# Twelve key maxima and an expert's downward matmuls gathered at each gelu of the third feed-forward layer

## The chip, the cores and the metric

The kernel runs on one core of a Trainium2 chip. The metric is the time of one execution on the device, in microseconds (us). One core has TensorE (PE, matrix products), VectorE (DVE), ScalarE (ACT), GpSimd (POOL), and SyncE (SP), which here only issues DMA transfers. Each engine works through its own list of instructions in order; they meet at semaphores.

## The reference

Four layers are applied one after the other to 1024 tokens of width 128. Each has a cross attention over 6404 context rows (16 heads of 8 channels) and then a mixture of 8 experts, of which a token uses two:

```
x = x + attention_l(layernorm(x), context)      l = 0, 1, 2, 3
x = x + experts_l(layernorm(x))
attention: softmax(q k / sqrt(8)) v  for l = 0, 1, 3;  sigmoid(q k / sqrt(8)) v  for l = 2
experts, l = 2:
  comb = one_hot(top 2 of softmax(x @ router_w + router_b)), weighted
  for e in range(8):
      h = gelu(x @ expert_up[e].T)              # 128 -> 512, not approximate
      out = out + comb[:, e] * (h @ expert_down[e].T)
experts, l = 0, 1, 3: silu(x @ a) * (x @ b), then downward
```

## The kernel before

The tokens are cut into two blocks of 512, so there are 8 units of work: unit u is layer u // 2, block u % 2. The attention of a unit is done in 4 phases of 4 heads each, 32 phases in all. A phase walks over 51 tiles of 128 keys. For each key tile TensorE forms two score pairs (`score`, each two heads in two PSUM banks), ScalarE turns each pair into `prob` (`exp`: Exp, or Sigmoid in layer 2), and one tile later TensorE multiplies them with V (`av`, four heads). I count time in key tiles: a tile (24, 36) is tile 36 of phase 24, and its length is the time from its first `exp` to that of the next tile.

A softmax phase needs, beforehand, the maximum of each query's scores. These maxima of phase p + 1 are found during phase p: 176 pieces (`max` on TensorE into a bank of the three `side` banks, `red` on VectorE). 32 of them (`both`) work on a difference of two key chunks that TensorE and ScalarE prepared (`dif`, `relu`). They are handed out by `find`, which keeps a running sum of planned VectorE time (`spent`) in step with the position in the phase.

The experts of unit u - 1 are worked off as background while unit u attends. For layer 2 that is `pass_steps` with `gated` false: pass 4 (unit 4, during phases 20 to 22, Sigmoid, no maxima) and pass 5 (unit 5, during phases 24 to 26, Exp, with maxima). An expert k has four upward products (`up`, 128x512 out of Fin), each copied into a hidden buffer (`upc`: by VectorE in pass 4, where `by_dve` is true, by ScalarE in pass 5), a `gelu` over all four (one 128x2048 instruction, line 978), a multiplication with the routing weight on GpSimd (`hscale`, two instructions, line 1316, with the weight row in `cwb`), and four accumulating downward products (`down`, line 870), added up by `ysum` (in pass 5 by way of a ScalarE copy, `yc`). Two experts' gelus stand side by side, so that ScalarE loads the gelu table once for both and then loads its attention table again.

The order of all instructions is written out beforehand. `placed` gives every background step a position: a position is a quarter of a key tile, `gap` is the distance to the step before it, and a TensorE step takes a position of its own in each key tile, so eight `up` and eight `down` between two pairs of gelus take 16 tiles. `attention_steps` then lays scores, maxima and background steps into one list, and each engine takes its own steps from it in that order.

Weights: `wexp` fetches an expert's Fin and Fout (256 KB each, lines 1400 and 1401) into a ring of 3. The fetch for expert k + 3 waits until `down` of expert k has read its slot (line 1397), and `up` of expert k + 3 waits for it (line 847). `cwget` fetches the weight row of expert k + 2 into `cwb` once `hscale` of expert k is done (line 1413). Both are issued by SP, one after the other in the order of the list.

Of the kernel before, what the change touches and what calls it, by code (L numbers as in the profile page):

```python
# [7 lines left out]
ACT = mybir.ActivationFunctionType  # L8
# [29 lines left out]
E = 8  # L38
# [74 lines left out]
def softmax(l):  # L113
    return l != 2


def unit(u):

    return u // 2, u % 2
# [7 lines left out]
def by_dve(u, lp):  # L127

    return u in (3, 4, 7)
# [7 lines left out]
Step = namedtuple("Step", "eng what key")  # L137
# [138 lines left out]
def pass_steps(u, lp):  # L276

    l, b = unit(u)
    f = FFN[l]
    out = [(6, Step("PE", "logit", (u, lp)))]  # L280
    out += [(3 if what == "routea" else 2, Step("DVE", what, (u, lp))) for what in ("routea", "routeb", "routee", "routef", "routeg", "routeh")]
    out += [(2, Step("ACT", "rexp", (u, lp)))]
    out += [(4 if what == "routej" else 2, Step("DVE", what, (u, lp))) for what in ("routej", "routek", "routel")]
    if l == 0:
        out += [(2, Step("DVE", "routec", (u, lp))), (6, Step("PE", "count", (u, lp)))]
    out += [(2, Step("DVE", "routed", (u, lp))), (4, Step("PE", "cwT", (u, lp))), (1, Step("ACT", "cwTc", (u, lp))),
            (2, Step("SP", "cwput", (u, lp)))]
    for k in range(W_RING):
        out.append((0, Step("SP", "wexp", (u, lp, k))))
    out.append((0, Step("SP", "cwget", (u, lp, 0))))  # L290
    if f["gated"] and l != 3:
        out.append((0, Step("POOL", "xk", (u, lp, 0))))
    out.append((16, None))
    n = f["nk"]

    def down(k, c):
        out.append((1, Step("PE", "down", (u, lp, k, c))))
        if c == n - 1:
            if by_dve(u, lp):
                out.append((3, Step("DVE", "ysum", (u, lp, k))))  # L300
            else:
                out.append((0, Step("ACT", "yc", (u, lp, k))))
                out.append((0, Step("POOL", "ysum", (u, lp, k))))
            if k + W_RING < E:
                out.append((0, Step("SP", "wexp", (u, lp, k + W_RING))))

    def gated(k, j):
        out.append((1, Step("PE", "up", (u, lp, k, j))))
        out.append((0, Step("ACT", "tanh", (u, lp, k, j))))
        if l == 3 or not by_dve(u, lp):  # L310
            out.append((0, Step("ACT", "ac", (u, lp, k, j))))
        out.append((1, Step("PE", "up", (u, lp, k, n + j))))
        if by_dve(u, lp):
            out.append((2, Step("DVE", "gatea", (u, lp, k, j))))
            out.append((0, Step("DVE", "gateb", (u, lp, k, j))))
        else:
            out.append((0, Step("ACT", "gc", (u, lp, k, j))))
            out.append((0, Step("POOL", "gatea", (u, lp, k, j))))
            out.append((0, Step("POOL", "gateb", (u, lp, k, j))))
        if l == 3:  # L320
            out.append((0, Step("POOL", "gatec", (u, lp, k, j))))
        if j == 0 and k + 1 < E and l != 3:
            out.append((0, Step("POOL", "xk", (u, lp, k + 1))))

    if not f["gated"]:
        out.append((0, Step("SP", "cwget", (u, lp, 1))))
    for k in range(E):
        if f["gated"]:
            if k + 1 < E:
                out.append((0, Step("SP", "cwget", (u, lp, k + 1))))  # L330
            for j in range(n):
                gated(k, j)
            if k:
                for c in range(n):
                    down(k - 1, c)
            continue
        for j in range(n):
            out.append((1, Step("PE", "up", (u, lp, k, j))))
            out.append((3, Step("DVE", "upc", (u, lp, k, j))) if by_dve(u, lp) else (0, Step("ACT", "upc", (u, lp, k, j))))
            if k > 1:  # L340
                down(k - 2, j)
        if k % 2:
            out += [(0, Step("ACT", "gelu", (u, lp, i))) for i in (k - 1, k)]
            for i in (k - 1, k):
                out += [(0, Step("POOL", "hscale", (u, lp, i, j))) for j in range(2)]
                if i + 2 < E:
                    out.append((0, Step("SP", "cwget", (u, lp, i + 2))))
    out.append((8, None))
    for k in range(E - 1 if f["gated"] else E - 2, E):
        for c in range(n):  # L350
            down(k, c)
    out += [(6, Step("PE", "yT", (u, lp))), (3, Step("DVE", "yadd", (u, lp)))]
    return out
# [27 lines left out]
    return out  # L381


def placed(at, steps, taken):


    out = []
    for gap, s in steps:
        at += gap
        if s is not None and s.eng == "PE":  # L390
            at += (1 - at) % 4
            while at in taken:
                at += 4
            taken.add(at)
        if s is not None:
            out.append((at, s))
    return out


def loads(u):  # L400
# [3 lines left out]
    if b:  # L404
# [5 lines left out]
        if l == 3:  # L410
# [6 lines left out]
            ysum=0.7, upc=0.7)  # L417
# [5 lines left out]
def attention_steps(units):  # L423
# [4 lines left out]
    for p in range(first, last + 1):  # L428
        at = p * Q
# [13 lines left out]
    for u in units:  # L443
        at = NG * u * Q
        if u:
            back += placed(at + 16, finish_steps(u - 1), taken)
    for u in units:
        l, b = unit(u)
        at = NG * u * Q
# [5 lines left out]
    def window(p):  # L455

        return max(first * Q, (p - 1) * Q - LEAD), p * Q - LEAD

    out = []
    n = 0  # L460
    p = first + 1
    spent, single, both, ready, ahead, total = 0.0, [], [], [], [], None

    def find(half, t, most):

        nonlocal spent
        a, e = window(p)
        for _ in range(most):
            if t < e - 8 and spent >= total * (t + 1 - a) / (e - 8 - a):
                return  # L470
            if both[half] and (ready[half][0] <= t if ready[half] else False):
                i = both[half].pop(0)
                if both_of(ITEM_DIF[i])[1] == i:
                    ready[half].pop(0)
                spent += COST["both"]
            elif single[half]:
                i = single[half].pop(0)
                spent += COST["red"]
            else:
                return  # L480
            out.append(Step("PE", "max", (p, i)))
            out.append(Step("DVE", "red", (p, i)))

    for t in range(first * Q, (last + 1) * Q):
        kt, q = t // 4 % KT, t % 4
        if t >= window(p)[1]:
            assert total is None or not (single[0] or single[1] or both[0] or both[1] or ahead)
            p, total = p + 1, None
        has = p <= last + 1 and p < 32 and softmax(phase(p)[0]) and t >= window(p)[0]
        if has and total is None:  # L490
            a, e = window(p)
            half_of = len(HALVES[0])
            spent, single = 0.0, [list(range(0, half_of)), list(range(half_of, FIRST_BOTH))]
            both = [[i for i in range(FIRST_BOTH, len(ITEMS)) if ITEMS[i][2] // 2 == half] for half in range(2)]
            ready = [[], []]
            ahead = [(a + (e - 24 - a) * d // len(DIFS), d) for d in range(len(DIFS))]
            total = FIRST_BOTH * COST["red"] + (len(ITEMS) - FIRST_BOTH) * COST["both"]
            total += sum(COST.get(s.what, 0.15) for at, s in back if s.eng == "DVE" and a <= at < e - 8)
        if q in (0, 2):
            half = q // 2  # L500
            out.append(Step("PE", "score", (t // Q, kt, half)))
            out.append(Step("ACT", "exp", (t // Q, kt, half)))
            if has:
                find(1 - half, t, 2 if t < window(p)[1] - 8 else 5)
        if q == 3:
            if kt:
                out.append(Step("PE", "av", (t // Q, kt - 1)))
            elif t // Q > first:
                out.append(Step("PE", "av", (t // Q - 1, KT - 1)))
            if has:  # L510
                find(0 if len(single[0] + both[0]) > len(single[1] + both[1]) else 1, t, 1)
            if has and ahead and ahead[0][0] <= t and not ready[0] and not ready[1]:
                d = ahead.pop(0)[1]
                out.append(Step("PE", "dif", (p, d)))
                out.append(Step("ACT", "relu", (p, d)))
                ready[DIFS[d][1]].append(t + 5)
        while n < len(back) and back[n][0] <= t:
            s = back[n][1]
            out.append(s)
            if s.eng == "DVE":  # L520
                spent += COST.get(s.what, 0.15)
            n += 1
    out.append(Step("PE", "av", (last, KT - 1)))
    out.append(Step("ACT", "drain", (last,)))
# [1353 lines left out]
```

## Time and profile before

| | us |
|---|---|
| median of 3 runs | 4747.94 (4747.63 to 4750.8) |
| the profiled execution, its own time | 4733.75 |
| its span, first to last instruction | 4731.8 |
| TensorE busy | 3965.9 |
| ScalarE busy | 3983.6 |
| VectorE busy | 2803.3 |
| GpSimd busy | 829.8 |
| mean granted TensorE clock | 0.953 of full speed |

Busy times are unions over an engine's instructions. The time beside "span" is what a run of the kernel takes; the profiled execution was 14 us below the median of the three timed runs.

### The profile page before, as it was taken

What the parts mean: (1) busy time and instruction counts of PE and PEld (TensorE: products, weight loads), DVE (VectorE), ACT (ScalarE), POOL (GpSimd) and SP (SyncE); (2) the same over time, 40 slices, a digit from 0 to 9 for tenths busy, and PEclk for the clock granted to TensorE, in tenths of its full rate; (3) what the DMA queues carried; (4) which work ended last, traced back from release to release, by engine and by line L of the source; (5) the groups of instructions that cost most, each with busy time, mean ns of one, the idle gap of its engine ahead of it and who ended that gap; (6) DMA issues with size and microseconds to landing.
All of it is one profiled execution on the core that took longest, in us unless ns stands there. A gap on an engine that the chain in (4) does not pass through costs nothing. (4 is left out here: it accounts for less than half of the span.)

```text
span 4731.8 us, 68983 instructions
## 1 busy us (share of the span) xinstructions
PE 3965.9 (84%) x26742; PEld 911.7 (19%) x26742; DVE 2803.3 (59%) x5598; ACT 3983.6 (84%) x4403; POOL 829.8 (18%) x719
## 2 busy tenths in 40 slices
PE   3578888888888888888898999888888888888887
PEld 2112111111112221122112222111111111122112
DVE  1487888778877778877610111011287568886833
ACT  2478998889978898888899888978998888888994
POOL 3001000340014410143522011012001120035002
PEclk7579999999989999999999999999999999999998
DMA  2212000110002110011102121100001100011001
GB/s 73 84 42 56 20 13 18 31 29 10 13 26 56 30 47 10 19 47 35 37 13 61 37 74 40 35 31 26 13 13 36 32 13 13 14 32 32 10 1 47
DMA packets 105922, 150.33 MB, mean 32 GB/s; under 512 B 23064, under 2 KB 64032, under 8 KB 105584
## 3 DMA queue, kind: packets, MB, share of 16 engines
q1 hardware_dynamic: 105584, 145.82, 10.9%
q8 instruction: 213, 3.49, 0.3%
q14 instruction: 125, 1.02, 0.1%
HBM read 122.24 MB, written 23.51 MB: 31 GB/s over the span
## 5 line engine op out<-in xcount | busy, mean ns | idle before, releaser
L913 ACT ACTIVATE prob<-scores 128x1024 f32<-128x1024 f32 x3264 | 3177.3, 1025 | 274.4 <-PE scores L748 259.6
L1022 DVE TENSOR_REDUCE mpart<-side 128x1 f32<-128x512 f32 (+1 forms) x3312 | 2039.4, 656 | 707.8 <-PE side L779 697.5
L758 PE MATMUL av<-prob,VB 128*9 128x512 f32 x6528 | 873.3, 607 | 1.3 <-ACT prob L913 0.5
L758 PE MATMUL av<-prob,VA 128*9 128x512 f32 x6528 | 869.5, 605 | 1.7 <-ACT prob L913 0.8
L748 PE MATMUL scores<-QP,KA 32*128 32x512 f16 x3264 | 640.7, 393 | 195.2 <-ACT above L921 118.2
L748 PE MATMUL scores<-QP,KB 32*128 32x512 f16 x3264 | 630.5, 388 | 195.0 <-ACT above L921 94.2
L779 PE MATMUL side<-KB,QP 32*128 32x512 f16 (+1 forms) x2112 | 583.8, 385 | 43.0 <-DVE mpart L1022 29.1
L779 PE MATMUL side<-KA,QP 32*128 32x512 f16 (+1 forms) x1936 | 534.0, 378 | 33.3 <-DVE mpart L1022 19.4
L1026 DVE CUSTOM_DVE_ANT_0 above<-side,above 128x512 f32<-128x512 f32 x736 | 493.0, 685 | 69.9 <-PE side L779 68.1
L921 ACT ACTIVATE above<-scores 128x1024 f32<-128x1024 f32 x368 | 376.8, 1024 | 169.1 <-PE scores L770 118.1
L748 PEld LDWEIGHTS scores<-QP,KB 32*128 32x128 f16 x3264 | 151.8, 91 | 867.7 <-ACT prob L913 538.6
L748 PEld LDWEIGHTS scores<-QP,KA 32*128 32x128 f16 x3264 | 151.8, 91 | 818.8 <-ACT prob L913 437.0
L779 PEld LDWEIGHTS side<-KB,QP 32*128 32x128 f16 x2112 | 140.2, 91 | 591.3 <-DVE mpart L1022 452.5
L779 PEld LDWEIGHTS side<-KA,QP 32*128 32x128 f16 x1936 | 130.8, 91 | 522.2 <-DVE mpart L1022 389.3
L852 PE MATMUL scores<-xnT,Fin 128*128 128x512 f32 (+1 forms) x256 | 147.5, 659 | 45.1 <-ACT above L921 31.7
L870 PE MATMUL side<-hT,Fout 128*128 128x512 f32 (+1 forms) x304 | 172.1, 653 | 8.0 <-POOL hT L1316 4.2
L1233 POOL TENSOR_TENSOR o_tok<-o_tok,bvo 128x512 f32<-128x512 f32 x6 | 7.6, 1272 | 890.5 <-DVE o_tok L1054 491.3
L1294 POOL TENSOR_TENSOR ag<-ag 128x512 f32<-128x512 f32 (+1 forms) x80 | 101.5, 1269 | 330.2 <-ACT ag L967 330.2
L1343 POOL CAST hi<-kb 128x512 f16<-128x512 f32 (+1 forms) x60 | 35.7, 596 | 626.3 <-ACT kb L997 625.8
L1524 DVE TENSOR_REDUCE mpart<-side 128x1 f32<-128x512 f32 (+1 forms) x80 | 49.3, 633 | 144.6 <-PE side L1476 144.6
L758 PEld LDWEIGHTS av<-prob,VA 128*9 128x9 f32 x6528 | 96.9, 88 | 192.4 <-issue 184.8
L758 PEld LDWEIGHTS av<-prob,VB 128*9 128x9 f32 x6528 | 97.0, 88 | 192.0 <-issue 184.5
(200 smaller groups left out, 2787.3 us busy)
## 6 DMA issues: line engine op xcount, KB each, us to landing
cwb<-weights SPq DMA_DIRECT2D x80, 256.0 KB, 3.8
KA<-kstacks SPq DMA_DIRECT2D x192, 96.0 KB
KB<-kstacks SPq DMA_DIRECT2D x192, 96.0 KB
Fin<-in_Fin SPq DMA_DIRECT2D x64, 256.0 KB, 2.8
kstacks<-hi SPq DMA_DIRECT2D x112, 128.0 KB, 2.4
ctxc<-in_ctxT SPq DMA_DIRECT2D x48, 256.0 KB, 3.0
kstacks<-lo SPq DMA_DIRECT2D x56, 128.0 KB, 2.6
hT<-in_mask SPq DMA_DIRECT2D x16, 400.2 KB, 3.3
```

Of the source, the lines that this page charges most:

```text
L748: last = pe.matmul(pair[:, j, :], K[p % 2][rows(h), kt * P:kt * P + P], QP[p % 3][rows(h), :], start=True, stop=True)
L758: last = pe.matmul(AV[ROWS * h:ROWS * h + VC, :], V[l % 2][:, kt, g * HG + h, :], prob[:, (e + h // 2) % RING, (h % 2) * QB:(h % 2) * QB + ...
L779: pe.matmul(bank[:, 0:chunk_of(c)], QP[p % 3][rows(h), qt * P:(qt + 1) * P], K[p % 2][rows(h), chunk(c)], start=True, stop=True).then_inc( ...
L852: pe.matmul(bank[0:fs, :], Fin[:, w, j * fs:(j + 1) * fs], x[:], start=True, stop=True).then_inc(sem["bgP"], 1)
L870: pe.matmul(bank, Fout[0:fs, w, c, :], h, start=first, stop=c == nk - 1).then_inc(sem["bgP"], 1)
L913: act.activation(prob[:, e % RING, :], pair.rearrange("p a b -> p (a b)"), ACT.Exp if softmax(l) else ACT.Sigmoid, scale=SCALE).then_inc(s ...
L921: act.activation(above[:].rearrange("p a b -> p (a b)"), pair.rearrange("p a b -> p (a b)"), ACT.Relu).then_inc(sem["bgA"], 1)
L1022: dve.tensor_reduce(part, bank, AX.X, ALU.max).then_inc(sem["red"], 1)
L1026: dve.tensor_tensor_reduce(more, bank, more, 1.0, LEAST, ALU.add, ALU.max, part).then_inc(sem["red"], 1)
L1294: pool.tensor_tensor(a, a, g, ALU.mult).then_inc(sem["bgG"], 1)
L1343: pool.tensor_copy(hi16[:, slot, 0:w], k).then_inc(sem["bgG"], 1)
L1524: dve.tensor_reduce(mpart[:, qt, h, c:c + 1], MX[:, n_max % 2, 0:chunk_of(c)], AX.X, ALU.max).then_inc(sem["red"], 1)
```

## The change

Three things are changed in the written order; no instruction is added or taken away, and no tile or buffer changes. First, after a pair of gelus the `down` products of expert k - 2 are placed at the same position as the gelus (`SAME`), behind them, where they had been spread among the `up` of expert k. Second, in pass 4 (`by_dve`) the four `up` of expert k + 1, with their copies, are placed there too, behind those `down`, and the `down` of expert k - 1 then follow one per key tile. Third, after each gelu at a time when maxima are being looked for (pass 5) six maxima are handed out at once, three from each half of the heads, whatever the running sum says.

```diff
-    def down(k, c):
-        out.append((1, Step("PE", "down", (u, lp, k, c))))
+    def down(k, c, gap=1):
+        out.append((gap, Step("PE", "down", (u, lp, k, c))))
         if c == n - 1:
             if by_dve(u, lp):
-                out.append((3, Step("DVE", "ysum", (u, lp, k))))
+                out.append((3 if gap > 0 else 0, Step("DVE", "ysum", (u, lp, k))))
...
-        for j in range(n):
-            out.append((1, Step("PE", "up", (u, lp, k, j))))
-            out.append((3, Step("DVE", "upc", (u, lp, k, j))) if by_dve(u, lp) else (0, Step("ACT", "upc", (u, lp, k, j))))
-            if k > 1:
-                down(k - 2, j)
+        if k % 2 or not k or not by_dve(u, lp):
+            for j in range(n):
+                out.append((1, Step("PE", "up", (u, lp, k, j))))
+                out.append((3, Step("DVE", "upc", (u, lp, k, j))) if by_dve(u, lp) else (0, Step("ACT", "upc", (u, lp, k, j))))
+                if k % 2 == 0 and k:
+                    down(k - 2, j)
         if k % 2:
             out += [(0, Step("ACT", "gelu", (u, lp, i))) for i in (k - 1, k)]
             for i in (k - 1, k):
                 out += [(0, Step("POOL", "hscale", (u, lp, i, j))) for j in range(2)]
                 if i + 2 < E:
                     out.append((0, Step("SP", "cwget", (u, lp, i + 2))))
+            if k > 1:
+                for j in range(n):
+                    down(k - 2, j, SAME)
+            if k + 1 < E and by_dve(u, lp):
+                for j in range(n):
+                    out += [(SAME, Step("PE", "up", (u, lp, k + 1, j))), (0, Step("DVE", "upc", (u, lp, k + 1, j)))]
+                for j in range(n):
+                    down(k - 1, j)
...
+SAME = -1
...
     for gap, s in steps:
+        if gap == SAME:
+            out.append((at, s))
+            continue
         at += gap
...
-    def find(half, t, most):
+    def find(half, t, most, now=False):
...
-            if t < e - 8 and spent >= total * (t + 1 - a) / (e - 8 - a):
+            if not now and t < e - 8 and spent >= total * (t + 1 - a) / (e - 8 - a):
                 return
...
             if s.eng == "DVE":
                 spent += COST.get(s.what, 0.15)
+            if s.what == "gelu" and has:
+                find(0, t, 3, True)
+                find(1, t, 3, True)
```

## Rows read from the trace of the kernel before

**Rows 1.** The page, part 1, and part 5: engine, operation, tiles, count | busy us, mean ns | idle before it.
```profile
PE 3965.9 (84%) x26742; PEld 911.7 (19%) x26742; DVE 2803.3 (59%) x5598; ACT 3983.6 (84%) x4403; POOL 829.8 (18%) x719
...
L1022 DVE TENSOR_REDUCE mpart<-side 128x1 f32<-128x512 f32 (+1 forms) x3312 | 2039.4, 656 | 707.8 <-PE side L779 697.5
```
**Rows 2.** Timeline of TensorE in pass 4: start, length, line, tiles, count, idle before.
```profile
3196.57 1.13 PE L852 MATMUL side<-xnT,Fin 128*128 128x512 f32 x2
3197.63 0.39 PE L748 MATMUL scores<-QP,KB 32*128 32x512 f16 x2
3197.95 1.05 PE L758 MATMUL av<-prob,VA 128*9 128x512 f32 x8
3198.93 0.39 PE L748 MATMUL scores<-QP,KB 32*128 32x512 f16 x2
3199.25 1.12 PE L870 MATMUL side<-hT,Fout 128*128 128x512 f32 x2
```
**Rows 3.** Timeline of ScalarE in phase 22, where no expert steps are.
```profile
3318.25 77.36 ACT L913 ACTIVATE prob<-scores 128x1024 f32<-128x1024 f32 x83
```
**Rows 4.** Windows: length, busy of `exp`, PEclk, DMA, GB/s; pass 4, none, pass 5.
```profile
3072.80:3094.20 21.40, 16.39 (x17) 1.00 0.11 38
...
3542.70:3599.10 56.40, 42.51 (x45) 1.00 0.15 49
3706.30:3753.60 47.30, 30.32 (x30) 1.00 0.10 30
```
**Rows 5.** Timeline of ScalarE at the second pair of gelus of pass 4.
```profile
3146.19 1.28 ACT L978 ACT_TABLE_LOAD   x1
3147.49 1.91 ACT L978 ACTIVATE tx<-tx 128x2048 f32<-128x2048 f32 x1
3149.30 1.90 ACT L978 ACTIVATE hT<-hT 128x2048 f32<-128x2048 f32 x1
3151.22 1.28 ACT L913 ACT_TABLE_LOAD   x1
3152.51 2.85 ACT L913 ACTIVATE prob<-scores 128x1024 f32<-128x1024 f32 x3
```
**Rows 6.** Timeline of TensorE there.
```profile
3144.72 0.39 PE L748 MATMUL scores<-QP,KB 32*128 32x512 f16 x2
3147.33 1.10 PE L852 MATMUL side<-xnT,Fin 128*128 128x512 f32 x2 [2.22 <-DMA Fout<-in_Fout]
...
3153.59 0.61 PE L748 MATMUL scores<-QP,KB 32*128 32x512 f16 x2 [2.96 <-ACT prob L913]
3154.12 1.90 PE L758 MATMUL av<-prob,VA 128*9 128x512 f32 x8
```
**Rows 7.** Timelines of GpSimd and of SP's DMA issues there.
```profile
3149.47 4.65 POOL L1316 TENSOR_TENSOR tx<-tx,cwb 128x1024 f32<-128x1024 f32 x2 [41.12 <-ACT tx L978]
3154.09 4.65 POOL L1316 TENSOR_TENSOR hT<-hT,cwb 128x1024 f32<-128x1024 f32 x2
...
3143.52 0.36 SPq L1400 DMA_DIRECT2D Fin<-in_Fin  x1
3143.92 0.44 SPq L1401 DMA_DIRECT2D Fout<-in_Fout  x1
3154.15 4.94 SPq L1416 DMA_DIRECT2D cwb<-weights  x2
```
**Rows 8.** Windows, `exp` alone, over the four pairs of gelus of pass 4.
```profile
3094.20:3105.80 11.60, 5.27 (x5) 0.71 0.09 21
3145.20:3160.90 15.70, 7.16 (x7) 0.78 0.15 53
3202.00:3212.20 10.20, 5.12 (x6) 0.83 0.12 43
3253.20:3268.00 14.80, 7.23 (x8) 0.77 0.00 0
```
**Rows 9.** The same over the four pairs of pass 5.
```profile
3623.40:3641.30 17.90, 7.43 (x7) 0.81 0.12 30
3692.10:3706.30 14.20, 5.38 (x5) 0.76 0.20 57
3753.60:3768.40 14.80, 5.42 (x6) 0.77 0.16 53
3813.70:3834.00 20.30, 9.14 (x9) 0.66 0.00 1
```
**Rows 10.** Timeline of TensorE and VectorE at the third pair of gelus of pass 5.
```profile
3762.88 0.61 PE L748 MATMUL scores<-QP,KB 32*128 32x512 f16 x2 [6.24 <-ACT prob L913]
...
3763.79 2.07 PE L852 MATMUL scores<-xnT,Fin 128*128 128x512 f32 x2 [0.30 <-ACT above L921]
...
3755.23 1.29 DVE L1022 TENSOR_REDUCE mpart<-side 128x1 f32<-128x512 f32 x2 [0.33 <-PE side L779]
```
**Rows 11.** Windows with a low granted clock: PE, PEld, DVE, ACT, POOL busy, PEclk, DMA.
```profile
3153.20:3160.10 6.90, 6.51 (x24) 1.06 (x24) 0.00 (x0) 4.14 (x5) 5.54 (x3) 0.51 0.14 47
...
3818.80:3832.50 13.70, 8.79 (x39) 1.33 (x39) 4.55 (x7) 9.81 (x9) 9.27 (x4) 0.50 0.00 1
```

## The prediction

> **What bounds the kernel now.** The page's first part shows TensorE and ScalarE both busy 84% of the span and VectorE 59% [rows 1], so the bound has to be read stage by stage. I went from the page to the timelines of ScalarE, TensorE and SP around the gelus, and then to windows for the rate of the regular stretches. No other stage is touched.
>
> In pass 4 a key tile with one expert product takes 21.4 us / 8 = 2.67 us (8 tiles in the first window of [rows 4]). The reader is to see in the timeline that TensorE has no gap: 1.06 (product) + 0.32 + 0.98 + 0.32 us [rows 2]. It is the bound there. Without a product ScalarE sets the pace: 83 `exp` in 77.36 us, so 1.86 us per tile [rows 3]. Each expert product that leaves a tile is therefore worth 2.67 - 1.86 = 0.81 us. In pass 5 a tile takes 47.3 / 15 = 3.15 us with a product and 56.4 / 22 = 2.56 us without (15 and 22 tiles in [rows 4]; a count there may hold one `exp` cut off at the edge), so 0.59 us per product.
>
> A pair of gelus keeps ScalarE away from the attention for 3152.51 - 3146.19 = 6.32 us [rows 5]. TensorE runs out of work meanwhile: it idles 2.22 us for weights and then 2.96 us for ScalarE [rows 6], 6.24 us in pass 5 [rows 10]. When it resumes, the granted clock is at 0.50 to 0.51, that is 1.2 instead of 2.4 GHz [rows 11], and an expert product takes 2.07 us where it took 1.12 us [rows 10, 2].
>
> **What moves.** Pass 4 places 12 `up` (experts 2, 4, 6) and 12 `down` (1, 3, 5) at the gelus, pass 5 places 12 `down`. Gain in the stretches: 24 x 0.81 = 19.4 us and 12 x 0.59 = 7.1 us, 26.5 us together. What it costs is how much longer each of the eight holes becomes. I set T = 0 at the start of the gelu's table load. ScalarE can resume at T = 6.3, and it needs the next score pair, which stands in TensorE's list behind everything that was moved.
>
> **Pass 4, experts 0 and 1.** TensorE is free at T = -1.1 (score ends 3145.11, load 3146.19 [rows 5, 6]). Four `up` take 4.2 us, to 3.1. The next step is now `down` 0, in the same tile, and waits for `hscale`, which starts at T = 3.28 and takes 2.33 [rows 7], to 5.6; then `down` 6.7, score 7.0, `av` 8.0, next tile's score 8.3. The tile takes 9.4 us; I add 1.0 us for a low clock that may follow the gap of 2.5 us. Before: 11.6 us for two tiles [rows 8], less one regular 2.67, 8.9. Cost 1.5 us.
>
> **Pass 4, experts 2 and 3, and 4 and 5: the step that decides.** Behind the gelus now stand `down` 1, then `up` 4. `up` 4 needs the weights whose fetch waits for `down` 1, and that fetch is issued by SP. Before, it stood ahead of the gelus: `down` 1 was done, SP issued Fin at 3143.52, and `up` 4 ran at 3147.33, 3.81 us later [rows 6, 7]. In the new list SP first meets the two `cwget` of experts 4 and 5, and the second waits for the last `hscale` of expert 3. GpSimd needs four times 2.33 us from T = 3.28, and the second cwb issue ends at 3154.15 + 4.94 = 3159.09, T = 12.9 [rows 7]. Only then can the weights be issued: they land at T = 16.7, though `down` 1 was done at T = 3.1. Four `up` take 4.2 us plus 2.3 us, since the clock will be low after 13.6 us of idling (about 4.5 us of it at half speed, as behind the other holes [rows 6, 11]): 23.2. `down` 2, score, `av`, score: 26.0. Everything else in TensorE's list, the attention's scores above all, is queued behind that `up`, and ScalarE waits for them from T = 6.3. The tile takes 27.1 us. Before: 15.7 - 2 x 2.67 = 10.4 us and 10.2 - 2.67 = 7.5 us [rows 8]. Cost 16.7 and 19.6 us. Bounds: without the low clock 2.3 us less each; with a landing 1.5 us later (the cwb transfer beside it) and the clock low throughout, 4 us more each.
>
> **Pass 4, experts 6 and 7.** Four `down` fill T = -1.1 to 3.1, nothing waits for them. 14.8 us [rows 8] become 8.3 + 1.9 + 2.7 and 0.6 for the clock, 13.5: cost -1.3 us.
>
> Pass 4 sums to 1.5 + 16.7 + 19.6 - 1.3 - 19.4 = 17.1 us slower.
>
> **Pass 5.** Twelve maxima behind the gelus go through three banks, so VectorE sets their pace: two in 1.29 us with one fill, 0.61 us apart [rows 10]. TensorE issues the twelfth at about T = 6. With nothing behind it (experts 0 and 1) the score comes at 6.4, just in time. What is gained is that 12 maxima are missing from the next tiles and the clock may hold: before, three tiles took 17.9 us where 9.5 is regular [rows 9, 4]; I take -2 us (0 to -4).
>
> At the other three pairs the four `down` follow, their bank free at T = 6.3, and end at 10.5, or 11.4 with some low clock. ScalarE's list has `yc` right behind the gelus, which waits for them, and then the table load and the `exp`: 11.9, 13.2. ScalarE was due at 6.3, and the next tile starts at T = 14.1 instead of 8.1. That 6 us is given back in part by fewer maxima and the missing slow tiles (14.2 us for two, 20.3 for four [rows 9]): cost 3.5 us at the second pair, 3.1 at the last. At the second and third pair the weights again land at T = 17, which `up` waits for, two tiles behind at the second pair (the transposes at the phase's end come between) and one tile behind at the third: 2.4 and 4.9 us more. Sum: -2 + 5.9 + 8.4 + 3.1 - 7.1 = 8.3 us. Nearest rows of both signs give 0 to 18.
>
> The Trainium skill has a rule that weighs on the other side. "TensorE: Matmul & The Clock Gate", part 1, says that the clock gate follows how busy the array is, so filled holes would keep 2.4 GHz. The trace agrees that the clock falls behind the idle holes [rows 11]; that is the fourth rival below. A second one speaks against the change. "ScalarE: Activation LUTs", section "What ACT_TABLE_LOAD costs", adds a drain of about 1.38 us to the 1.28 us of each load, and behind `yc` that load now stands on the path at three pairs of pass 5. The trace differs: the `exp` starts 1.29 us after its load and the first gelu 1.30 us after its own [rows 5]. By the rule those pairs would cost 4 us more, an estimate of 4777 us.
>
> **Sum.** 17.1 + 8.3 = 25.4 us. The profiled execution (4733.75 us, span 4731.8) would become 4759; it lies 14 us below the median of the runs, 4747.9, to which I add the same: **4773 us**, slower by 0.5%. Order alone changes, so no other term exists than waits and clock.
>
> **Rivals.**
> 1. *SP's list does not hold the weights back* (the fetch only waits for `down`). They land at T = 3.1 + 3.8 = 7, `up` ends at 13.7 with the low clock, the tile takes 17.5 us: 9.6 us less at each of the two pairs, and 3 us less in pass 5. 25.4 - 22 = 3 us: 4751, no change. For it: a median transfer of 3.8 us; against it: the order of the list and lines 1397 and 1413.
> 2. *More low clock.* After such idling the low stretch lasts as after the last gelu, 13.7 us [rows 11], not 6.9. TensorE-bound tiles then cost up to 1.3 us more, five to six per hole in three or four holes: 4795.
> 3. *Moved waits appear at other places too*, in the chain of the maxima at the end of phase 24, where the second pair of pass 5 now falls; 5 us more, 4778.
> 4. *The other side: the holes swallow the work.* If the weights are there when `up` 4 comes and TensorE keeps 2.4 GHz from the gelu to the next score, a hole with eight products takes 11 us instead of 17.5, and of the gain of 26.5 us some 20 stay: 4728, faster. It decides from the point at which the weights land before T = 4. For it: TensorE idles 6.2 us per hole; against it: even unhindered, eight products are 8.5 us of work and twelve maxima and four products 10.5, in a hole of 7.4.
>
> **Chances.** Forecast 0.66, rival 1 0.15, rivals 2 and 3 0.10, rival 4 0.09. The 80% range is 4750 to 4796, from rival 1's price to rival 2's. 0.2% (9.5 us) is about what a measurement of this kernel can tell. Faster: rival 4, 0.09. Within: rival 1 and the low tail of the forecast, 0.16. Slower: 0.75.
>
> **What would show it.** In the changed kernel: at the second and third pair of gelus of pass 4 TensorE idles 12 to 14 us in one piece, ended by the DMA of Fout, and SP issues Fin right behind the second cwb. ScalarE has one idle time of 17 us or more before an `exp` there. The 16 tiles between gelus are 8. In pass 5 the gelu's `yc` comes 5 to 6 us behind the second gelu, and the attention's table load behind it. Wrong would be: Fin issued before cwb, a gap of TensorE of 4 us or less, or the clock at 1.00 through the holes.

## The result, and the profile after

The changed kernel takes 4774.95 us (median, 4761.75 to 4787.01), the kernel before 4737.81 (4725.36 to 4750.8) in the same comparison. The ratio is 1.0068, 95% interval 1.0044 to 1.0092: slower by 21 to 44 us. The profiled execution has a span of 4771.1 us, against 4731.8.

The page of the kernel after (parts 1 and 5, as in [rows 1]) shows the same work and hardly more busy time:

```profile
PE 3979.9 (83%) x26742; PEld 920.0 (19%) x26742; DVE 2800.3 (59%) x5598; ACT 3978.2 (83%) x4403; POOL 829.7 (17%) x719
...
L1041 DVE TENSOR_REDUCE mpart<-side 128x1 f32<-128x512 f32 (+1 forms) x3312 | 2036.9, 657 | 694.5 <-PE side L798 684.3
```

ScalarE is busy 5 us less and TensorE 14 us more, and the kernel is 39 us longer: what was added is waiting. All line numbers after are 19 higher (`exp` 932, `gelu` 997, `up` 871, `down` 889).

**Pass 4, second pair.** Timelines of ScalarE and of TensorE, kernel after, where [rows 5, 6] stood before (start, length, line, tiles, count, idle before):

```profile
3137.27 1.28 ACT L997 ACT_TABLE_LOAD   x1
3138.56 1.91 ACT L997 ACTIVATE tx<-tx 128x2048 f32<-128x2048 f32 x1
3140.38 1.89 ACT L997 ACTIVATE hT<-hT 128x2048 f32<-128x2048 f32 x1
3142.29 1.28 ACT L932 ACT_TABLE_LOAD   x1
3161.64 1.02 ACT L932 ACTIVATE prob<-scores 128x1024 f32<-128x1024 f32 x1 [18.07 <-PE scores L767]
...
3136.11 3.70 PE L889 MATMUL side<-ag,Fout 128*128 128x512 f32 x8
3155.21 5.21 PE L871 MATMUL side<-xnT,Fin 128*128 128x512 f32 x8 [15.40 <-DMA Fout<-in_Fout]
3160.26 1.02 PE L889 MATMUL side<-tx,Fout 128*128 128x512 f32 x2
3161.21 0.39 PE L767 MATMUL scores<-QP,KA 32*128 32x512 f16 x2
```

The four `down` are done at once, then TensorE idles 15.40 us in one piece until the weights land, and ScalarE has nothing for 18.07 us. Why they land late stands in the timelines of GpSimd and of SP there (before: [rows 7]):

```profile
3140.55 4.64 POOL L1335 TENSOR_TENSOR tx<-tx,cwb 128x1024 f32<-128x1024 f32 x2 [24.16 <-ACT tx L997]
3145.16 4.63 POOL L1335 TENSOR_TENSOR hT<-hT,cwb 128x1024 f32<-128x1024 f32 x2
...
3145.22 4.92 SPq L1435 DMA_DIRECT2D cwb<-weights  x2
3150.18 0.43 SPq L1419 DMA_DIRECT2D Fin<-in_Fin  x1
3150.65 0.43 SPq L1420 DMA_DIRECT2D Fout<-in_Fout  x1
```

`down` 1 had read the slot at 3139.8, but SP issues Fin at 3150.18, directly behind the second cwb, which itself waited for the last `hscale` (3149.8). The Trainium skill says the same of where such a wait sits ("DMA: Bandwidth & Descriptors", section "Anatomy of one DMA — SWDGE (gpsimd) path": a transfer's semaphore wait is done by the issuing engine ahead of dispatch). The section describes transfers that GpSimd issues; these rows, where SP issues them, agree: 10.4 us passed from the end of `down` 1 to the issue of Fin.

The windows over the four gelu pairs of pass 4 (`exp` alone; length, busy, PEclk, DMA, GB/s), before [rows 8]; the first holds two tiles, the next two hold one tile each, the last three:

```profile
3102.80:3118.10 15.30, 5.38 (x5) 0.78 0.11 25
3136.20:3162.90 26.70, 3.33 (x3) 0.74 0.16 40
3184.00:3210.70 26.70, 3.30 (x3) 0.74 0.14 40
3235.40:3251.30 15.90, 7.24 (x8) 0.79 0.00 0
```

**Pass 5, third pair.** The same windows over the tiles with the gelus, one tile each (before, such a tile stood in [rows 9] with the slow ones behind it), and ScalarE, TensorE and VectorE at the third:

```profile
3652.00:3663.30 11.30, 3.34 (x4) 0.71 0.03 9
3699.60:3716.60 17.00, 3.33 (x3) 0.80 0.11 33
3765.70:3782.10 16.40, 3.33 (x3) 0.79 0.09 25
3826.70:3842.50 15.80, 3.15 (x3) 0.78 0.00 0
```
```profile
3767.38 1.28 ACT L997 ACT_TABLE_LOAD   x1
...
3778.38 0.60 ACT L1002 ACTIVATE yb<-side 128x512 f32<-128x512 f32 x1 [6.00 <-PE side L889]
3778.99 1.28 ACT L932 ACT_TABLE_LOAD   x1
3780.29 1.02 ACT L932 ACTIVATE prob<-scores 128x1024 f32<-128x1024 f32 x1
...
3769.64 3.59 PE L798 MATMUL side<-KA,QP 32*128 32x512 f16 x6 [0.21 <-DVE mpart L1041]
3773.22 5.12 PE L889 MATMUL side<-hT,Fout 128*128 128x512 f32 x8
3778.28 0.39 PE L767 MATMUL scores<-QP,KB 32*128 32x512 f16 x2
...
3785.59 2.05 PE L871 MATMUL scores<-xnT,Fin 128*128 128x512 f32 x2 [3.83 <-DMA Fout<-in_Fout]
...
3767.70 6.66 DVE L1041 TENSOR_REDUCE mpart<-side 128x1 f32<-128x512 f32 x11
```

Eleven maxima in a row take VectorE 6.66 us, one per 0.61 us; TensorE follows them through the banks, the four `down` start at T = 5.8 (T = 0 is the table load, 3767.38), `yc` runs at T = 11.0 after 6.00 us of idling, and only behind it the table load. A tile later `up` waits for weights.

Where the time went, from the first `exp` of one phase to that of another in the two profiled executions: phases 20 to 22 with pass 4 take 410.0 us against 390.1 (19.9 us longer), phases 23 to 27 around pass 5 take 736.3 against 727.3 (9.0 us longer), and 8.7 us lie ahead of phase 20, where the order is the same. So one pair of profiles is not enough to price a pass. Four profiles have pass 4 in the order of before (390.1 us here, and 398.7, 400.5 and 400.5 in e3, e8 and e11 below) and three have it in the order of the change (410.0, and 417.3 and 415.1 in e4 and e5). The means differ by 16.7 us. For phases 23 to 27 there are two of each: 727.3 and 723.3 (e4) against 736.3 and 744.1 (e8), 14.9 us. Together that is 31.6 us, where the runs give 32.

### The profile page after: what moved, and what is told of

It is laid out like the page before. It is cut to its first block and busy times, and to the rows that moved or that the text cites. A ratio compares the mean times of both kernels' runs of the same rounds, so it can differ in the third digit from the quotient of the medians.

```text
span 4771.1 us, 68981 instructions
## 1 busy us (share of the span) xinstructions
PE 3979.9 (83%) x26742; PEld 920.0 (19%) x26742; DVE 2800.3 (59%) x5598; ACT 3978.2 (83%) x4403; POOL 829.7 (17%) x719
## 5 line engine op out<-in xcount | busy, mean ns | idle before, releaser
L798 PE MATMUL side<-KA,QP 32*128 32x512 f16 (+1 forms) x1936 | 535.5, 378 | 37.3 <-DVE mpart L1041 24.1
L871 PE MATMUL side<-xnT,Fin 128*128 128x512 f32 x192 | 105.7, 660 | 42.3 <-DMA Fout<-in_Fout 41.7
```

The lines of the kernel that those rows point to most:

```text
L798: pe.matmul(bank[:, 0:chunk_of(c)], QP[p % 3][rows(h), qt * P:(qt + 1) * P], K[p % 2][rows(h), chunk(c)], start=True, stop=True).then_inc( ...
L871: pe.matmul(bank[0:fs, :], Fin[:, w, j * fs:(j + 1) * fs], x[:], start=True, stop=True).then_inc(sem["bgP"], 1)
```

## The experiments

Each was compared with the kernel before on the same chip. Ratios to the kernel before:

| kernel | median us | before | ratio, 95% interval |
|---|---|---|---|
| the change | 4774.95 | 4737.81 | 1.0068 (1.0044 to 1.0092) |
| e1_weights_first | 4748.13 | 4741.22 | 1.0019 (1.0010 to 1.0029) |
| e2_weights_behind | 4788.44 | 4741.22 | 1.0111 (1.0094 to 1.0128) |
| e3_maxima_alone | 4743.58 | 4741.22 | 1.0013 (1.0000 to 1.0027) |
| e4_pass4_alone | 4759.18 | 4741.22 | 1.0040 (1.0026 to 1.0054) |
| e5_yc_behind_exp | 4773.29 | 4745.16 | 1.0061 (1.0041 to 1.0082) |
| e8_pass5_alone | 4764.19 | 4740.25 | 1.0042 (1.0028 to 1.0057) |
| e11_downs5_alone | 4746.88 | 4740.25 | 1.0008 (0.9995 to 1.0020) |
| e6_fill_behind_score | 4716.20 | 4745.16 | 0.9947 (0.9926 to 0.9968) |
| e7_fill_and_maxima | 4709.27 | 4745.16 | 0.9930 (0.9911 to 0.9950) |
| e10_weights_in_time | 4701.64 | 4745.16 | 0.9917 (0.9896 to 0.9939) |
| e9_in_time_no_maxima | 4693.39 | 4740.25 | 0.9901 (0.9888 to 0.9915) |

**e1_weights_first: the changed kernel with the fetch of weights ahead of the two cwget in SP's list.**

```diff
                 out += [(0, Step("POOL", "hscale", (u, lp, i, j))) for j in range(2)]
-                if i + 2 < E:
-                    out.append((0, Step("SP", "cwget", (u, lp, i + 2))))
             if k > 1:
                 for j in range(n):
                     down(k - 2, j, SAME)
+            out += [(SAME, Step("SP", "cwget", (u, lp, i + 2))) for i in (k - 1, k) if i + 2 < E]
```

> The changed kernel with one difference: at a pair of gelus SP's list has the weights' fetch (wexp) ahead of the two cwget, not behind them. Theory (SP issues in order, so the weights are held back by the wait for hscale): at the second and third pair of gelus of pass 4 the weights land at about T = 7 to 8 instead of 17.9, the tile falls from 26.7 us to about 16, 10 us less each; at the third pair of pass 5 up 4 no longer waits (3 to 4 us less). 22 to 25 us less than the changed kernel in all, so within 12 us of the kernel before. Rival (eight products are simply too much for a hole; the order of SP does not matter): tiles stay at 26 to 27 us, the time stays at that of the changed kernel, 1.007 of before.

The loss falls from 0.68% to 0.19%, some 23 us, by moving two issues of SP and nothing else. TensorE and ScalarE at the second pair of pass 4 (their table load is at 3127.30):

```profile
3133.60 5.37 PE L870 MATMUL side<-xnT,Fin 128*128 128x512 f32 x8 [3.75 <-DMA Fout<-in_Fout]
...
3140.19 1.02 ACT L931 ACTIVATE prob<-scores 128x1024 f32<-128x1024 f32 x1 [6.58 <-PE scores L766]
```

The idle time of 15.40 us is 3.75 and the tile 15.2 us instead of 26.7. SP's issues there:

```profile
3129.88 0.33 SPq L1418 DMA_DIRECT2D Fin<-in_Fin  x1
...
3135.26 4.93 SPq L1434 DMA_DIRECT2D cwb<-weights  x2
```
The fetch still starts only when `down` 1 is done, so the weights come at T = 6.3, and ScalarE waits 6.58 us. Phases 20 to 22 are then 0.7 us shorter than in the profile before, and 8 us shorter than the mean of the four profiles with that order; phases 23 to 27 are still 9.1 us longer, though the tile in which `up` waits at the third pair of pass 5 falls from 8.2 to 4.5 us, as expected. This is the prediction's deciding step, shown, and rival 1 disproved: the list of SP is what held the weights.

**e2_weights_behind: the kernel before, with only that order of SP.**

```diff
-            if k + W_RING < E:
+            if k + W_RING < E and (f["gated"] or k % 2 == 0):
                 out.append((0, Step("SP", "wexp", (u, lp, k + W_RING))))
...
+            if k > 1 and k + 1 < E:
+                out.append((0, Step("SP", "wexp", (u, lp, k + 1))))
```

> The kernel before with one difference: at the pairs of gelus with weights to fetch (two in pass 4, two in pass 5) SP's list has the fetch behind the two cwget. TensorE's order is that of the kernel before. Theory: up of experts 4 and 6 waits until T = 17 with the score behind it; the tile grows from 8.3 to about 20 us in pass 4, and the next tile by about 9 us in pass 5: 35 to 40 us slower than before (1.008), as slow as the whole change or slower. Rival (the loss comes from the moved products): no more than 2 us.

Worse than the change itself: 47 us by the medians, 53 by the ratio. TensorE at the second pair of pass 4:

```profile
3175.48 2.05 PE L854 MATMUL side<-xnT,Fin 128*128 128x512 f32 x2 [19.18 <-DMA Fout<-in_Fout]
```

No product and no maximum is moved here; SP's order alone makes gelu tiles of 24.1 and 23.6 us. The expectation of 35 to 40 us was too low by some 10 us. I had expected the tiles at about 20 us and the weights at T = 17. They come about 1 us later, and the trace has stretches of low clock of 23.9 and 20.5 us there. That these make up the rest is not shown.

**e3_maxima_alone: the kernel before, with the six maxima at each gelu.**

```diff
+            if s.what == "gelu" and has:
+                find(0, t, 3, True)
+                find(1, t, 3, True)
```

> The kernel before with the six maxima behind each gelu alone. Theory: the twelve end at T = 6.0 to 6.4, when ScalarE comes back, so they cost nothing and take work from later tiles: 0 to 8 us faster. Rival (VectorE is slower and holds the score back, or the clock falls all the same): 0 to 6 us slower.

Ratio 1.0013 (1.0000 to 1.0027): no gain. VectorE and TensorE at the first pair of pass 5 and ScalarE behind it, then the window of low clock there (PE, PEld, DVE, ACT, POOL busy, PEclk, DMA):

```profile
3627.22 7.27 DVE L1025 TENSOR_REDUCE mpart<-side 128x1 f32<-128x512 f32 x12 [0.72 <-PE side L782]
...
3629.76 0.39 PE L782 MATMUL side<-KB,QP 32*128 32x512 f16 x1 [0.21 <-DVE mpart L1025]
...
3636.18 1.02 ACT L924 ACTIVATE above<-scores 128x1024 f32<-128x1024 f32 x1 [1.33 <-PE scores L773]
```
```profile
3631.30:3641.50 10.20, 9.30 (x30) 1.31 (x29) 3.18 (x6) 7.03 (x7) 8.76 (x4) 0.50 0.14 30
```

TensorE runs a maximum of 0.39 us in every 0.60, and the clock falls to 0.50 all the same, for 10.2 us where the idle hole before had 6.8. I had put -2 us on this pair for a clock that holds. The Trainium skill ("TensorE: Matmul & The Clock Gate", part 1) has the gate follow how busy the array has been, from which I had taken that a filled hole keeps 2.4 GHz. This trace does not bear that out for a hole filled in this way.

**e4_pass4_alone and e8_pass5_alone: each half of the change.** In e4, pass 5 keeps the order of before and there are no maxima at the gelus. The edit of the changed kernel:

```diff
-                if k % 2 == 0 and k:
+                if k > 1 and (k % 2 == 0 or not by_dve(u, lp)):
                     down(k - 2, j)
...
-            if k > 1:
+            if k > 1 and by_dve(u, lp):
                 for j in range(n):
                     down(k - 2, j, SAME)
...
-            if s.what == "gelu" and has:
-                find(0, t, 3, True)
-                find(1, t, 3, True)
```

e8 has the two conditions the other way round (`not by_dve` at the second), keeps the maxima, and no `up` is moved.

> The changed kernel's order in pass 4 alone; pass 5 and the maxima as before. Theory: two thirds of the loss is here, 17 to 20 us slower than before (1.004), with the two tiles of 26.7 us. Rival (the two passes share the loss otherwise, or it comes from the maxima): under 8 us.

> The change's pass 5 alone: the four downward products of expert k - 2 behind each pair of gelus of pass 5, and the six maxima at each gelu; pass 4 is in its order of before. The whole change costs 32 to 33 us in the runs and its pass 4 alone cost 18 us. If the two halves add up, this kernel costs 10 to 15 us (ratio 1.002 to 1.003), with gelu tiles of pass 5 of 15 to 17 us and yc about 11 us behind the table load. Rival: the loss in pass 5 comes only because pass 4 shifts it against the phases' clocks; then the kernel is within 3 us of before.

By the ratios e4 costs 19 us (12 to 26) and e8 20 us (13 to 27). Together 39, where the whole change costs 32: they add up within their intervals. So e4 came out as expected (17 to 20 us). For pass 5 I had predicted only 8.3 us and then expected 10 to 15 of e8, too little. The gelu tiles of e8 are 11.3, 17.1, 16.3 and 15.8 us, as in the change.

**e5_yc_behind_exp: the change, with `yc` placed a position later, behind the next `exp`.**

```diff
-                out.append((0, Step("ACT", "yc", (u, lp, k))))
+                out.append((0 if gap > 0 else 1, Step("ACT", "yc", (u, lp, k))))
```

> The changed kernel with one difference: in pass 5 the yc of the gathered down stands behind the next exp in ScalarE's list, not ahead of it and of its table load. Theory (yc keeps the table load on the path): the load follows the gelus at once, the exp comes 1.9 us earlier at three pairs, 5 to 6 us less than the changed kernel, not more, since the score itself is behind the maxima and the down. Rival (yc is what costs in pass 5): the three tiles of 15.8 to 17 us fall to 10, 15 us less.

29 us slower than before by the ratio, where the change was 32; the intervals overlap, so a gain isn't shown. ScalarE at the third pair:

```profile
3783.05 1.28 ACT L932 ACT_TABLE_LOAD   x1
3789.59 1.02 ACT L932 ACTIVATE prob<-scores 128x1024 f32<-128x1024 f32 x1 [5.25 <-PE scores L767]
```

The table load is out of the chain, but the `exp` waits 5.25 us: its scores stand in TensorE's list behind the same maxima and products. So `yc` was the symptom. The three gelu tiles are 15.3, 15.5 and 15.6 us here against 17.0, 16.4 and 15.8 in the change: not the 10 us of the rival, and the 5 to 6 us that I had expected in all are not shown either.

**e11_downs5_alone: e8 without the maxima.** The edit takes the three lines of e3 out of e8.

> As e8_pass5_alone, but without the six maxima at each gelu. Theory: the twelve maxima ahead of the downward products are what delays yc and the attention's scores, since the products wait for banks that VectorE empties one per 0.6 us. Without them the four products run at T = 0 to 4 us, yc stands directly behind the gelus, the gelu tiles fall from 16 us to 8 to 9.5 us, and the kernel is 3 to 8 us faster than before (12 x 0.59 gained, 2 to 4 us given back by up waiting for weights whose fetch stands behind two cwget). Rival: the fetches behind the cwget are the cost in pass 5; then it is 3 to 8 us slower than before, with waits of up for Fout of 5 us and more.

Ratio 1.0008 (0.9995 to 1.0020): of the 20 us of e8, 16 go with the maxima. Alone they had cost little or nothing (e3); they cost here because the four `down`, and the score behind them, stand behind them in TensorE's list. ScalarE and TensorE at the third pair (table load at T = 0 as before):

```profile
3757.77 1.28 ACT L988 ACT_TABLE_LOAD   x1
...
3762.68 0.58 ACT L993 ACTIVATE yb<-side 128x512 f32<-128x512 f32 x1
3763.28 1.28 ACT L923 ACT_TABLE_LOAD   x1
3764.57 1.02 ACT L923 ACTIVATE prob<-scores 128x1024 f32<-128x1024 f32 x1
...
3756.96 3.60 PE L880 MATMUL side<-hT,Fout 128*128 128x512 f32 x8
...
3775.82 2.04 PE L862 MATMUL scores<-xnT,Fin 128*128 128x512 f32 x2 [9.78 <-DMA Fout<-in_Fout]
```

The reader is to see both mechanisms in one place. `yc` follows the gelus with no wait and the gelu tile is 10.3 us (16.4 in the change, 10.0 before). But a tile later `up` waits 9.78 us for weights (3.83 in the change): the late fetch was there all along, landing at T = 18 in both, and the maxima had covered part of it. The theory is right on what delayed `yc` and wrong on the sum (faster by 3 to 8 us). The rival's waits are there, and its price of 3 to 8 us fits the 3.8 us of the ratio, though the interval doesn't exclude that nothing is lost.

**e6, e7, e10, e9: the holes filled in the right order.** Here the four products stand not at the gelu but behind that tile's second score and `av` (position 3 of the tile), so that ScalarE's next work is ahead of them, and the cwget stand behind the weights' fetch. In pass 4 these are `up` of the next expert (the `down` that frees their weights now stands among the `up` ahead of the gelus), in pass 5 `down` of expert k - 2. So 28 products are moved, four to a hole, where the change moved 36 and put eight into a hole in pass 4:

```diff
+        if gap < 0:
+            at += (3 - at) % 4 if gap == FILL else 0
+            out.append((at, s))
+            continue
...
+            if ahead and k + 1 < E:
+                out += gets
+                for j in range(n):
+                    out += [(SAME if j else FILL, Step("PE", "up", (u, lp, k + 1, j))), (SAME, Step("DVE", "upc", (u, lp, k + 1, j)))]
+            else:
+                if k > 1:
+                    for j in range(n):
+                        down(k - 2, j, SAME if j else FILL)
+                out += gets
```

> Another order: four products per pair of gelus, placed behind the score and av of the gelu's own tile (what ScalarE needs when it is back), the weights' fetch ahead of the cwget or of the gelus; no maxima are gathered. Pass 4 moves up 2, 4, 6 and down 5, pass 5 moves down 1, 3, 5. Theory (moving pays when nothing that ScalarE waits for stands behind it, and weights are there): the gelu tiles stay at 8.3 us in pass 4 and 10 in pass 5, 16 x 0.81 + 12 x 0.59 = 20 us less, and some 0 to 10 us of low clock: 20 to 30 us faster than before (0.995). Rival (any product behind a gelu costs what it saves): within 5 us of before.

e7 adds four maxima at that place ahead of the four `down` (eight where there are none), with `now`:

```diff
+        if t == burst and has:
+            for half in range(2):
+                find(half, t, 2 if filled else 4, True)
```

> The order of e6 with maxima at the same place in pass 5: four ahead of the four down, eight where no down follows. Theory: VectorE is not the bound in these tiles, so little is gained: 0 to 5 us less than e6. Rival (VectorE's idle 6 us per pair are worth having): 10 us less than e6.

e10 is e7 with every `down` that frees a weight slot two products earlier against the `up` it releases:

```diff
+MIXED = ([UP[0], DOWN[0], DOWN[1], UP[1], DOWN[2], DOWN[3], UP[2], UP[3]],
+         [DOWN[0], DOWN[1], UP[0], DOWN[2], UP[1], DOWN[3], UP[2], UP[3]],
+         UP)
```

> The order of e7, and between the gelus the down of expert k stand two products further ahead of the up of expert k + 3, whose weights their end releases. Theory: the waits for weights of 2 us of TensorE and 2 to 4 us per tile at five places go, and the low clock behind them: 8 to 15 us less than e7. Rival (the transfer is hidden already): no difference.

e9 is e10 without e7's lines:

> e10_weights_in_time without the four or eight maxima at each gelu of pass 5, all else the same. Theory: with the products behind the tile's second score, the maxima at the gelus still give what e7 gave over e6, 5 to 9 us: this kernel then takes 4706 to 4711 us (ratio 0.9925 to 0.9935). Rival: the maxima give nothing of their own (as e3 says of them alone); then it takes 4698 to 4704 us, as e10 does (ratio 0.991 to 0.9925).

All four are faster than the kernel before. e6 gains 25 us by the ratio, as expected (20 to 30). e9, the best, gains 0.99% (0.85 to 1.12%), 46.9 us. e7 over e6 looked like 7 us for the maxima, but their intervals overlap, and e9 against e10 shows none: without them it is not slower. I had expected e9 at 4706 to 4711 us; the rival (nothing of their own) stands, as in e3, though 4693.39 lies below its 4698 to 4704 too. What the earlier `down` are worth was expected at 8 to 15 us. e10 over e7 gives 6 us by the ratios, with intervals that overlap, so it isn't shown there. e9 over e6 is the same step without maxima: 22 us by the ratios (0.9901 against 0.9947), and these intervals don't overlap. ScalarE and TensorE of e10 at the second pair of pass 4:

```profile
3133.72 1.28 ACT L1012 ACT_TABLE_LOAD   x1
...
3140.04 2.86 ACT L947 ACTIVATE prob<-scores 128x1024 f32<-128x1024 f32 x3
...
3132.78 1.05 PE L792 MATMUL av<-prob,VA 128*9 128x512 f32 x8
3133.75 3.70 PE L886 MATMUL side<-xnT,Fin 128*128 128x512 f32 x8
3137.39 0.39 PE L782 MATMUL scores<-QP,KB 32*128 32x512 f16 x2
```

The four `up` start with the table load, wait for nothing, run at 2.4 GHz, and the next score is in PSUM at T = 4.1, before ScalarE can want it. The gelu tile takes 8.28 us, as it did before without them. In the stretch from 3090 to 3960 us the granted clock is low for 58 us in e6, 55 in e7, 51 in e10 and 48 in e9, and for 99 before, 102 after the change and 106 to 140 in e1 to e5, e8 and e11.

These four orders differ from the change in three ways at once: the next score stands ahead of the products, their weights come in time, and there are four products to a hole, not eight. What weights in time are worth is seen in e1 and in e9 over e6. The other two are not separated: no run puts eight products behind the score.

## Why the prediction held, and where it was off

Predicted 4773.0, measured 4774.95. The agreement is in part luck: a cost that I sized too small and a base that was too high nearly cancel. I added 25.4 us to a median of 4747.94; in the comparison the kernel before was at 4737.81, and the ratio gives 32 us (21 to 44). The difference was under-estimated by 7 us (12 by the medians), and the base that I took over was 10 us too high. By the profiles of same order, pass 4 cost 16.7 us where I had 17.1, and pass 5 cost 14.9 where I had 8.3. The mechanism of pass 4 was right and the one wrong size is pass 5's.

Of the signs that I named, SP issued Fin right behind the second cwb, ScalarE idled 18.07 us before an `exp`, the 16 tiles between gelus of pass 4 became 8 or 9, and `yc` came 6.00 us behind the second gelu with the table load behind it. TensorE's idle time of 15.40 us lies outside the 12 to 14 that I gave.

- **The regular tiles.** 2.67 us with a product and 1.86 without: unchanged after.
- **Pass 4, the two middle pairs, the step that decides.** Predicted a tile of 27.1 us, measured 26.72 and 26.73. Inside it two errors cancel: the weights landed at T = 17.9, not 16.7 (5.0 us after Fin's issue, where [rows 6, 7] had 3.81), and the four `up` took 5.05 us, not 6.5, since most of the low clock (13.7 us from 3144.7) passed while TensorE idled. Four products in a row also take 3.70 us at full clock (the `down` at 3136.11), where I had counted 4.2. e1 and e2 show the mechanism from both sides.
- **Pass 4, first and last pair.** Predicted cost 1.5 and -1.3 us. Two tiles took 15.3 us, less one regular tile 12.6, against 8.9: cost 3.7. The last three took 15.9 us, not 13.5, against 14.8: cost 1.1. With both, the sum of my terms in this profile is 3.7 + 16.3 + 19.2 + 1.1 - 19.4 = 20.9 us, against 19.9 by its phases. In e4 and e5, with the same order of pass 4, the first gelu tile is 9.57 us and the next one 2.67, so the extra 3 us at the first pair are a stretch of low clock that falls there (3110.5 to 3117.3) and not always.
- **Pass 5, first pair.** Predicted -2 for a clock that holds. Three tiles took 18.5 us against 17.9, and e3 finds no gain. This step failed: a run of maxima paced by VectorE does not hold the clock.
- **Pass 5, the other pairs.** Predicted the next tile at T = 14.1, measured 14.7 (3782.11 - 3767.38), with `yc` at 11.0, and the weights one tile behind costing 4.53 us of ScalarE's time where I had 4.9. The whole of pass 5 costs 14.9 us by the two profiles of each order, and 20 (13 to 27) by e8's runs, against my 8.3. The step that was sized too small is the cost of each pair. The three late gelu tiles grew by 6.7, 6.4 and 6.8 us where I had 6, and less of it came back: over five tiles from the gelu's, the first pair cost 0.4 us (e8: 1.6), the third 10.4 (10.4) and the last 4.5 (4.6), where I had -2, 8.4 and 3.1. The second can't be compared so, since it now falls at a phase's end. These three alone are 5.8 us more (e8: 7.1) than I had.
- **The rival that the clock stays low longer** (4795): its condition came true and its price did not. At both middle pairs of pass 4 the low stretch is 13.7 us long (from 3144.7 and from 3192.4), as it had assumed, but TensorE was idle for most of each. The 102 us of low clock against 99 before don't settle the sum: in phases 20 to 22 the four profiles with the order of before have 34, 58, 61 and 61 us, the three with that of the change 48, 72 and 68.
- **The chain of maxima at the end of phase 24:** no run was made for it; open.
- **The holes swallow the work** (4728, 0.09): wrong for this order, right in part for another. Its condition, weights there when `up` 4 comes, can't be met while `down` 1 runs in the same hole: even with SP's list in order they came at T = 6.3 (e1). Once the release is moved out of the hole and the next score ahead of the products, e9 gains 47 us. By my prices its 28 products are worth 16 x 0.81 + 12 x 0.59 = 20 us. The rest goes with the waits for weights that it removes and with the low clock, which halves; no run separates these two. This was with four products to a hole; whether eight can be swallowed is open.
- **The table load behind `yc`.** The `exp` starts 1.30 us after its load (3778.99, 3780.29). The drain of 1.38 us that the Trainium skill adds ("ScalarE: Activation LUTs", section "What ACT_TABLE_LOAD costs") is not seen here either. In the profile before, each of the 24 loads starts within 0.02 us of the end of the instruction ahead of it, and the next starts 1.29 us after the load.

## What to carry to other kernels

Work moved into an engine's idle hole goes behind the last thing that ends the hole for the other engine, and nothing in it may wait: look up who frees what it reads, and move that release ahead of the hole. A transfer has the time of its place in the issuing queue, not of its own condition; waits ahead of it on SP cost 11.5 us per gelu tile here (26.7 against 15.2) and some 50 us by themselves (e2). When several things are gathered at once, time each alone: here the maxima, the part meant to fill the hole, cost 16 of pass 5's 20 us, though alone they cost little or nothing. And price a pass from several profiles of the same order, not from one pair.

## What the runs showed of the hardware that I had not expected

- TensorE issuing a maximum of 0.39 us every 0.60 us fell to half clock in e3 (3631.3, for 10.2 us), as from an idle hole.
- The low clock runs on through idle time: in a hole of 15.4 us the stretch of 13.7 us was nearly over when work came (3144.7 to 3158.4, work from 3155.21), and the four products took 5.05 us against 3.70 at full clock, less than the 6.5 predicted.
- Right behind a cwb transfer, the two fetches of an expert had landed, and `up` ran, 5.0 us after the first was issued (3150.18 to 3155.21); alone it was 3.8 us ([rows 6, 7]).
- Where the order is the same, profiled executions differ by where the clock is low: phases 20 to 22, unchanged, are 8.6 us longer in e3 and 10.4 in e8 and e11 than in the profile before. A term below that is not to be read from one profile.
